# An fp32 product of a scan's front divided by batches, one half of it moved ahead among the transposes

## The reference, cut to what matters

```python
h = _L0_tok_ref(x, emb_weight, conv_weight)        # relu(conv(embedding)), 8 x 512 x 128
h = h + _L0_attn_ref(_layernorm(h), init_states, A, B, C, D)
h = h + _L0_ffn_ref(_layernorm(h), ...)            # 8 experts, 128 -> 512 -> 128
# inside _L0_attn_ref: a scan over the tokens with a constant A
#   x_t = x_(t-1) A + u_t B,   4 heads of 64 states,   y = scaled x C + u D
```

## Time and profile before

| what | value |
|---|---|
| median of three runs | 172.16 us (171.99 to 172.4) |
| profiled execution, its own time | 172.16 us |
| its span in the trace | 170.4 us |
| TensorE busy, TensorE weight loads busy | 160.6 us (94%), 137.8 us (81%) |
| VectorE, ScalarE, GpSimd busy | 130.5, 101.0, 101.5 us |

### The profile page before, as it was taken

One profiled execution on the slowest core, in us unless ns is written; L12 is line 12 of the kernel. 1 busy time (PEld: TensorE's weight loads), 2 busy tenths in 40 slices (PEclk: granted clock), 3 DMA queues, 4 the chain that ended last, 5 costly groups with the idle time before them and its releaser, 6 DMA issues.

```text
span 170.4 us, 3456 instructions
## 1 busy us (share of the span) xinstructions
PE 160.6 (94%) x1149; PEld 137.8 (81%) x1149; DVE 130.5 (77%) x403; ACT 101.0 (59%) x236; POOL 101.5 (60%) x168
## 2 busy tenths in 40 slices
PE   5987989998999999999999989999999999989992
PEld 1676875896666789987679889999999999989991
DVE  3979959735548375897995998989989898649893
ACT  3048999362124532323436857958779587788991
POOL 4437777659997035361223594896978969785000
PEclk9999999999999999999999999999999999999999
DMA  5995000000000000000000000010010100110022
GB/s 138 391 427 254 6 0 2 0 6 0 0 0 0 4 0 0 0 6 0 0 0 0 0 4 0 0 67 0 0 67 0 63 0 4 62 62 2 4 104 83
DMA packets 2182, 7.47 MB, mean 44 GB/s; under 512 B 238, under 2 KB 748, under 8 KB 1908
## 3 DMA queue, kind: packets, MB, share of 16 engines
q1 hardware_dynamic: 2146, 7.23, 11.1%
q10 hardware_dynamic: 18, 0.02, 0.1%
HBM read 5.15 MB, written 2.10 MB: 43 GB/s over the span
## 4 chain that ended last, share of the span: by engine, by line
PE 79%; POOL 6%; ACT 5%; DVE 4%; issue 3%; DMA 2%; ACTq 0%; POOLq 0%
PE bank L1308 12%; PE bank L1288 12%; PE bank L1237 8%; PE bank L1152 6%; PE bank L1146 5%; PE bank L1083 4%; PE bank L1234 4%; PE bank L1033 4%; PE bank L1257 4%; PE bank L1089 4%; PE bank L1114 2%; PE bank L1264 2%; POOL rstd L517 2%; PE bank L1058 2%; PE bank L1006 2%
## 5 line engine op out<-in xcount | busy, mean ns | idle before, releaser
L534 POOL TENSOR_TENSOR hid_p<-hid_f,hid_p 128x256 fp32r<-128x256 f32 x48 | 34.1, 735 | 13.8 <-ACT hid_p L684 13.8
L682 ACT ACTIVATE hid_f<-bank,pa 128x256 f32<-128x256 f32 x64 | 30.8, 491 | 15.9 <-PE bank L1288 14.2
L1288 PE MATMUL bank<-xaT_p,fc_p 128*128 128x256 f32 x192 | 35.0, 293 | 0.2 <-issue 0.2
L1308 PE MATMUL bank<-hid_p,out_hi 128*128 128x256 f32 x128 | 32.5, 290 | 1.0 <-POOL hid_p L534 1.0
L1288 PEld LDWEIGHTS bank<-xaT_p,fc_p 128*128 128x128 f32 x192 | 26.7, 189 | 0.4 <-issue 0.3
L1308 PEld LDWEIGHTS bank<-hid_p,out_hi 128*128 128x128 f32 x128 | 23.4, 188 | 2.0 <-POOL hid_p L534 1.4
L684 ACT ACTIVATE hid_p<-bank,pa 128x256 fp32r<-128x256 f32 x48 | 23.4, 487 | 0.0
L1237 PE MATMUL bank<-pb,xh 128*128 128x128 f32 x128 | 19.5, 275 | 0.0
L517 POOL TENSOR_TENSOR rstd<-spread,neg_half 128x8 f32<-128x8 f32 x8 | 13.6, 1697 | 9.5 <-DVE spread L943 9.5
L1308 PE MATMUL bank<-hid_p,out_lo 128*128 128x256 f32 x64 | 17.8, 278 | 0.0
L1237 PEld LDWEIGHTS bank<-pb,xh 128*128 128x128 f32 x128 | 16.9, 192 | 0.0
(11 more groups left out here) (156 smaller groups left out, 373.6 us busy)
## 6 DMA issues: line engine op xcount, KB each, us to landing
fc_w<-in_fc SPq DMA_DIRECT2D x2, 2048.0 KB, 11.4
out<-res SPq DMA_DIRECT2D x7, 256.0 KB, 2.0
pa<-in_pack_a SPq DMA_DIRECT2D x1, 407.0 KB, 3.2
pb<-in_pack_b SPq DMA_DIRECT2D x1, 384.0 KB, 4.8
out<-res SPq DMA_DIRECT2D x2, 128.0 KB, 1.7
pw<-in_pack_a SPq DMA_DIRECT2D x1, 64.0 KB, 3.3
emb_w<-in_emb SPq DMA_DIRECT2D x1, 62.5 KB
conv_w<-in_conv ACTq DMA_DIRECT2D x1, 1.0 KB
```

Source lines behind the costliest of these rows:

```text
L534: nc.gpsimd.tensor_tensor(hid_p[1][:, half, c, :], hid_f[:, m % HID_SLOTS, :], hid_p[0][:, half, c, :].bitcast(F32), ALU.subtract).then_in ...
L682: full = nc.scalar.activation(hid_f[:, m % HID_SLOTS, :], src, ACT.Gelu, bias=bias)
L1288: last = mm(fc1_bank(8 * b + n)[:, 0:HALF], fc1_p[w][:, e * HID + c * P:e * HID + (c + 1) * P], xaT_p[m][:, b % 2, half, :], start=(k == 0 ...
L1308: last = mm(out_bank(b, half)[:, half * HALF:(half + 1) * HALF], out_p[w][:, e, c * CH:(c + 1) * CH], hid_p[m][:, half, c, :], start=(c == ...
```

## The change

Product a = 0 of group 0 is divided by batches. A new function `half_piece(half, q)` does one of its four matmuls for two batches (256 columns, in its half of bank 6). The half for batches 0 and 1 waits for `uT` of two batches instead of four and for five prepared products instead of six. Its four matmuls are issued one at a time in rounds 4 and 5: in each round one ahead of the transposes and one right behind them. The half for batches 2 and 3 is issued in round 6, where all four 512-column matmuls stood. Nothing changes on the other engines.

```diff
+        HALF_RUNS = {(4, 0): ((0, 0),), (4, 1): ((0, 1),), (5, 0): ((0, 2),), (5, 1): ((0, 3),)}
...
+                def half_piece(half, q):
+
+                    if q == 0:
+                        pe.wait_ge(uT_ready, GB // 2 * (half + 1))
+                        pe.wait_ge(prep_ready, N_LATE - 1)
+                    n = GB // 2 * half
+                    last = mm(scan_bank(0)[:, half * HALF:(half + 1) * HALF], b_then(0, RUN - 1 - q),
+                              u_runs(0, q)[:, n:n + GB // 2], start=(q == 0), stop=(q == RUN - 1))
+                    if half == 1 and q == RUN - 1:
+                        last.then_inc(run_done[0], 1)
...
                     for t in prep_tasks(b, 0):
                         prepare(t)
+                    for half, q in HALF_RUNS.get((b, 0), ()):
+                        half_piece(half, q)
                     if b >= 2:
                         transpose_u(b - 2)
+                    for half, q in HALF_RUNS.get((b, 1), ()):
+                        half_piece(half, q)
                     for t in prep_tasks(b, 1):
                         prepare(t)
-                    if b in (NB - 2, NB - 1):
+                    if b == NB - 2:
                         for q in range(RUN):
-                            run_piece(0, (b - (NB - 2)) * RUN + q)
+                            half_piece(1, q)
+                    if b == NB - 1:
+                        for q in range(RUN):
+                            run_piece(0, RUN + q)
```

## The result

| | before | after |
|---|---|---|
| median of five runs | 172.16 us (171.98 to 172.4) | 172.97 us (172.81 to 173.04) |
| span of the profiled execution | 170.4 us | 171.2 us |

The ratio of after to before is 1.005, with a 95% interval of 1.0038 to 1.0061.

The account below looks back on a forecast made before the run. Two chains meeting within 0.2 us end round 7: TensorE's own work, and ScalarE's relu copy of batch 6 followed by 5.5 us of VectorE. 1.72 added, 0.84 absorbed: 172.16 + 0.88 = 173.04, put at 173.0, range 172.2 to 173.6.

Parts of the forecast that it names:

- The price of a half product: On TensorE, 0.43 us each; eight more weight loads set at nothing, up to 0.3 us if each showed fully.
- Round 4: TensorE has no gap there; two half products make ScalarE's relu copy of batch 5 0.59 us late.
- Round 5: TensorE's gaps of 0.49 and 0.35 us are filled, absorbing 0.84 of 1.72; relu copy of batch 6 is 0.88 late.
- Rounds 6 and 7: TensorE's work ends at 29.84, VectorE's splits at 31.63, 0.88 late; 1.9 us of TensorE idle before a = 1.
- the label "issue": On 0.20 us of TensorE idle time before a = 1, read as a wait for VectorE's fourth split.
- Afterwards: From a = 1 to the end everything shifts by the same 0.88 us.
- the phase of attn_g: attn_g on VectorE beside a GpSimd subtraction: 0.8 us could come back or up to 0.5 go; taken as 0.
- The rule of the Trainium skill: VectorE and GpSimd share a port pair, held for a whole instruction; changed phase would matter, a common shift would not.
- The gain from filled gaps: Rival: TensorE ends round 7 0.84 us earlier and a = 1 follows if splits are not the limit: 171.3, chance 0.04.
- The general advice of the Trainium skill: Interleaving stretches with different limits may improve performance; worked out for this kernel as 171.3 us, chance 0.04.
- rival 2: At attn_g, VectorE and GpSimd part and 0.8 us comes back after the 0.88 delay: about 172.2, chance 0.06.
- The clock: Rival: TensorE's clock falls to 1.2 GHz after 1.9 us idle, doubling a = 1's twelve matmuls: about 175.6, chance 0.02.

Follow-up runs that it names:

- the second measurement: The changed kernel measured once more against the kernel before: 172.77 us beside 172.17, ratio 1.0030.
- The kernel with two in round 4: Against the changed kernel, only two half products are moved, to round 4; the other two stand in round 6: 172.56 us beside 172.16 for the kernel before.
- the kernel that has only these: Against the changed kernel, only two half products are moved, to round 5; the other two stand in round 6: 171.89 us, again 172.19.
- add without removing: Against the changed kernel, round 6 keeps its four whole products beside the half products in rounds 4 and 5: 172.79 us, ratio 1.0035 to the kernel before.
- remove without adding: Against the changed kernel, nothing stands in rounds 4 and 5 and three half products are left out of round 6: 171.94 us beside 172.07 before.
- the short chain: GpSimd copies high parts of batches 0 and 1 in rounds 4 and 5, VectorE makes their low parts earlier; on the kernel before: 171.83 us beside 172.07.
- The changed kernel with the short chain: The changed kernel with GpSimd making two high parts and VectorE two low parts earlier: 170.90 us beside 172.07 for the kernel before, again 171.41 beside 172.17.
- the one that leaves round 4 alone: Only two half products moved, to round 5, with GpSimd's early high parts and VectorE's early low parts: 170.95 us beside 172.07 before, again 171.05 beside 172.17.

## Why the prediction was right

**The number and the mechanism.** The forecast of 173.0 for a measured 172.97 is closer than the method allows: the second measurement gave 0.60 us of loss (0.28 to 0.77) instead of 0.81, and the time ahead of round 4 alone varies by more than such differences. What the prediction had right is the size of the delay from round 4 on, 0.88, and its path.

**The price of a half product.** Predicted 0.43 us each, and 0 to 0.3 for the additional weight loads, taken as 0. Measured 0.43, and 0.02 for all the loads. The bound of 0.3 doesn't follow from its own terms (eight times 0.1 are 0.8); it wasn't needed.

**Round 4.** Predicted: the transposes go from 19.57 to 20.00, ScalarE's copy of uT waits, the relu copy of batch 5 is 0.59 late. Measured, in profiles that are lined up (19.10 and 19.17, so 0.07 is to be added to a start of after): transposes at 20.01, relu copy at 22.24, 0.62 late. (The copy of uT of batch 1, which the prediction places by the earlier trace rows, isn't printed there; it starts at 17.36 in that timeline, ahead of the copy at 18.01, as was said.) The kernel with two in round 4 shows this step alone: 0.60 late at a = 1.

**Round 5.** Predicted: both gaps filled, 0.84 us absorbed, the relu copy of batch 6 0.88 late. Measured 0.87. That round 5 absorbs its own two products (0.04) is shown by the kernel that has only these.

**Rounds 6 and 7.** Predicted: a = 1 waits for VectorE's splits, which come 0.88 late as VectorE has no idle time to make it up; TensorE idles 1.9 us. Measured: 0.88 late, and 1.91 us of idle time on the weight path, 1.74 on the matmul path. ScalarE's relu copy of batch 7 was expected about 0.4 late and was 0.26 late (30.14 + 0.07 instead of 29.95), which costs nothing either way. The point on which the sign hung was the label "issue" at the earlier trace rows, which I read as a wait for the fourth split. The profile after writes the wait out, and the kernels that add without removing (12.56) and remove without adding (11.69) show it from both sides.

**Afterwards.** Predicted: the same shift to the end, with a bound of -0.8 to +0.5 for the phase of attn_g. Measured: 0.87 at the end, and attn_g at 1.04 instead of 1.09, 0.88 later. The place is as sensitive to phase as was said, since it gave back 0.37 us in the kernels with the short chain, but the change shifts both engines alike. The rule of the Trainium skill that was set beside it there ("SBUF — State Buffer", section "SBUF: two separate sides") agrees with the 0.70 us at another phase, as attn_g ends 0.08 us behind the subtraction in both. It doesn't fit every pair of rows of this case: the last section has a VectorE subtraction that wasn't held up by GpSimd.

**The rivals.** The gain from filled gaps (171.3) didn't come in this kernel, and it was said that it would need splits that end earlier. The short chain made them end earlier, and then it came. The general advice of the Trainium skill that was named with it ("Perfetto Trace Analysis", section "Optimization Strategy") gives no gain by itself here (a = 1 at 12.57 and 11.73 instead of 11.69); with VectorE's chain shortened the same moves gain (11.37 and 11.01). In the chances one piece doesn't add up: rival 2 gives 172.2, which is within 0.34 us of before, and yet its larger part was counted as faster. The clock didn't fall in the long wait: 1.00 from 30.0 to 31.6.

## What to carry to other kernels

In these runs a gap on the busiest engine was worth filling only where two things held, and they are worth checking elsewhere: what stands behind the gap in the same queue must feed no other chain that is already at its limit, and the place where the work is taken from must not be followed by a wait for another engine. The changed kernel with the short chain, whose two products in round 4 still delay VectorE, gained less (a = 1 at 11.37) than the one that leaves round 4 alone (11.01). Both can be read ahead of time, the first from who waits for the instructions behind the insertion point, the second from even 0.2 us of idle time in front of the next big group. Where two chains meet, shorten both and measure them together: here each alone was worth 0.12 and -0.04 us, and both 0.68.

## What the runs showed of the hardware

A power of 128x4 elements on GpSimd took 1.04 us alone and 1.37 or 1.53 beside a VectorE subtraction of two SBUF operands (128x512, 0.68 us). Two VectorE normalisations of 128x128 took 1.02 instead of 0.57 us beside a GpSimd copy of 128x512. But VectorE's subtraction L797 of 128x384 started at 28.26 and took 0.55 us while GpSimd's power (27.75 to 28.79) was still going. It wasn't held up: those of 128x256 and 128x512 behind it took 0.42 and 0.68, and 0.55 is between them. The small product behind that power then took 2.75 us instead of 0.20, beside five VectorE subtractions in a row, and ended at 31.61, 0.05 us behind the last of them:

```profile
27.75 1.04 POOL L482 TENSOR_TENSOR rstd<-tmp,neg_half 128x4 f32<-128x4 f32 x1
28.86 2.75 POOL L483 TENSOR_TENSOR tmp<-mv,rstd 128x4 f32<-128x4 f32 x1
```

These rows are of GpSimd's timeline after. So this power didn't keep VectorE out for all of its length, while the small product, by these times, got no turn until VectorE's subtractions were done. The subtraction of 128x512 on GpSimd, on the other hand, held attn_g up to its end, as told above.
